# Attention with seven of a quad's 64 blocks of exponentials taken as transposes of computed blocks

## The reference, cut to what matters

```python
heads = x.reshape(Bs, Ss, H, D)                      # H = 16, D = 8, Ss = 4096
qkv = _qz_ring(heads + rx_theta)
q = jnp.transpose(qkv, (0, 2, 1, 3))
scores = jnp.einsum('bhsd,bhtd->bhst', q, q) / np.sqrt(D)
attn = jax.nn.softmax(scores, axis=-1)
ctx = jnp.einsum('bhst,bhtd->bhsd', attn, q)
```

## Time and profile before

| | us |
|---|---|
| median of 3 runs | 8488.46 (8488.23 to 8497.59) |
| span of the profiled execution | 8347.0 |
| main stage, first to last exponential (of the span) | 595.3 to 8088.5 |
| ACT busy | 7572.6, 91% |
| PE busy | 7391.0, 89% |
| DVE busy | 3996.2, 48% |

### The profile page before, as it was taken

One profiled execution on the slowest core, in us unless ns is written; L12 is line 12 of the kernel. 1 busy time (PEld: TensorE's weight loads), 2 busy tenths in 40 slices (PEclk: granted clock), 3 DMA queues, 4 the chain that ended last, 5 costly groups with the idle time before them and its releaser, 6 DMA issues. The chain is left out here.

```text
span 8347.0 us, 169002 instructions
## 1 busy us (share of the span) xinstructions
PE 7391.0 (89%) x59247; PEld 2074.5 (25%) x59247; DVE 3996.2 (48%) x15349; ACT 7572.6 (91%) x6026; POOL 1120.4 (13%) x1165
## 2 busy tenths in 40 slices
PE   6558998889889999999999999999999988898987
PEld 3542221122212222222222222222222222121224
DVE  6984333333335555555555555555553343232553
ACT  2339999999999999999999999999999999999971
POOL 2742111111111111111111111111100000000000
PEclk8779999999999999999999999999999999999998
DMA  6752111111111111121112111111100010000018
GB/s 204 210 149 66 47 47 45 47 52 49 45 46 54 54 53 53 47 56 52 54 46 56 54 50 50 53 53 53 53 24 11 10 22 10 9 11 8 21 49 257
DMA packets 508316, 485.88 MB, mean 58 GB/s; under 512 B 229673, under 2 KB 411753, under 8 KB 506994
## 3 DMA queue, kind: packets, MB, share of 16 engines
q0 software_dynamic: 92880, 304.42, 12.5%
q1 hardware_dynamic: 414626, 170.83, 8.0%
HBM read 401.79 MB, written 73.33 MB: 57 GB/s over the span
## 5 line engine op out<-in xcount | busy, mean ns | idle before, releaser
L999 ACT ACTIVATE e<-sc 128x1536 f32<-128x1536 f32 x5376 | 7282.9, 1704 | 116.7 <-PE sc L928 115.4
L947 PE MATMUL acc<-e,v_cur 128*9 128x512 f32 x32256 | 4305.2, 598 | 30.5 <-DVE acc_sb L879 30.5
L928 PE MATMUL sc<-b_unit,a_cur 32*128 32x512 f16 x16384 | 2164.4, 386 | 544.6 <-ACT e L999 525.3
L928 PEld LDWEIGHTS sc<-b_unit,a_cur 32*128 32x128 f16 x16384 | 537.3, 91 | 4434.3 <-ACT e L999 4074.6
L605 POOL DMA_INDIRECT corners<-table,idx_st x873 | 835.0, 956 | 4728.4 <-ACT e L999 4417.2
L947 PEld LDWEIGHTS acc<-e,v_cur 128*9 128x9 f32 x32256 | 487.2, 89 | 974.9 <-issue 941.8
L629 DVE SCALAR_TENSOR_TENSOR val<-corners,w_st,val 128x128 f32<-128x128 f32 x2619 | 712.2, 345 | 7.7 <-DVE f_lg L1129 2.9
L879 DVE COPY acc_sb<-acc 128x512 f32<-128x512 f32 x129 | 89.1, 690 | 861.2 <-PE acc L947 843.4
L652 DVE TENSOR_TENSOR t_out<-misc,xt 128x128 f32<-128x128 f32 x96 | 28.0, 292 | 672.3 <-PE misc L708 637.1
L550 PE MATMUL cf_ps_t<-ident,cf_val 128*128 128x128 f32 x1152 | 160.0, 306 | 199.2 <-DVE cf_val L455 183.8
L416 POOL DMA_INDIRECT cf_corners<-table,cf_idx x288 | 285.2, 990 | 253.0 <-DVE cf_idx L441 148.5
(11 more groups left out here) (393 smaller groups left out, 4837.6 us busy)
## 6 DMA issues: line engine op xcount, KB each, us to landing
table<-pix SPq DMA_DIRECT2D x8, 2304.0 KB, 13.7
corners<-table,idx_st POOLq DMA_INDIRECT x873
ew<-in_ew SPq DMA_DIRECT2D x12, 1024.0 KB, 7.8
ew<-in_ew SPq DMA_DIRECT2D x48, 256.0 KB, 6.7
x_ch<-in_x SPq DMA_DIRECT2D x4, 2048.0 KB, 9.6
qn<-q SPq DMA_DIRECT2D x64, 128.0 KB, 2.5
ctx<-ctx_t SPq DMA_DIRECT2D x128, 64.0 KB, 1.8
out<-e_exp SPq DMA_DIRECT2D x32, 256.0 KB, 2.1
```

The lines of the kernel that those rows point to most:

```text
L928: last = self.nc.tensor.matmul(self.sc[k % self.SC][:, i, :], self.a[rows, t * P:(t + 1) * P], self.bst[u % 2][rows, :], start=True, stop= ...
L947: last = self.nc.tensor.matmul(self.acc[32 * h:32 * h + self.E1, :], self.v[:, t, h, :], self.e_of(j)[:, i, :], start=(t == 0), stop=(t == ...
L999: self.nc.scalar.activation(self.e_of(j)[:], self.sc[k % self.SC][:, 0:width, :], ACT.Exp, scale=1.0 / HD ** 0.5).then_inc(self.exp_done, 1)
```

## The change

For each quad, block (unit u, keys of chunk u+1), u = 0 to 6, is computed and kept, and block (unit u+1, keys of chunk u) is made from it and no longer computed. A new class `Plan` lays out the quad: 912 slabs in 304 steps of three, without tails; unit starts at steps 0, 43, 80, 118, 155, 192, 230, 267. The kept block is computed in two halves of three steps each (`e_kept`). `shuffle_sp` moves each half by 16 DMAs of 32 partitions x 8 slabs x 128 elements (128 KB) between quadrants into `e_turned`; `turn_dve` transposes it in 4 instructions of 128x1024 in 32x32 blocks, in place. Four turned groups stand at places 7, 9, 11 and 13 of the next unit's groups and read `e_turned` in runs of 32 elements. The ring of `e` has 5 buffers instead of 7. To make room, the convolution's weights and indices go to DRAM in the first stage and come back tile by tile (`rows_sp`), the `b` operand has one quad instead of two, and some buffers share memory. The items keep their order; `spread` maps their old positions to the new steps.

```diff
+    UNITS, PARTS, SC, WIDE, RING = UNITS, 4, 2, 3, 5
+    T_AT = (7, 9, 11, 13)
+            if u < UNITS - 1:
+                s0 = len(self.slabs)
+                n0 = next(n for n in ((9, 8, 7) if u else (3,)) if (s0 + 4 * n) % self.WIDE == 0)
+                kept = [self.GROUP * (u + 1) + t for t in range(self.GROUP)]
+                for i, n in enumerate((n0, 10)):
+                    order += left[:n]
+                    left = left[n:]
+                    self.halves[u, i] = (s0 + 4 * len(order)) // self.WIDE
+                    order += kept[2 * i:2 * i + 2]
+            order += left
+            self.slabs += [(u, t, h) for t in order for h in range(4)]
+            groups = [("direct", t) for t in order]
+            if u:
+                for bo, at in enumerate(self.T_AT):
+                    groups.insert(at, ("turned", bo))
...
+    def _before(self, k):
...
+            earlier = [k2 for k2 in self.slot if self.slot[k2] == self.slot[k]]
+        now = [k2 for k2 in earlier if k2 < k]
+        if now:
+            return self._last_use(max(now)) + 1
...
+    def spread(self, starts, old, items):
+        got, last = {}, -1
+        for at, item in sorted(items, key=lambda x: x[0]):
+            i, k = divmod(at, old)
+            if i + 1 < len(starts):
+                k = k * (starts[i + 1] - starts[i]) // old
+            k = max(last + 1, starts[i] + k)
...
+    def shuffle_sp(self, sp, qd, u, half):
+        done = qd * self.QUAD_STEPS + (self.plan.halves[u, half] + 3 + self.SC)
+        if half == 0:
+            used = self.plan.last_turned(u) + 1 if u else self.plan.last_turned(UNITS - 1) + 1 - UNITS * self.UNIT
+            sp.wait_ge(self.pv_done, qd * (UNITS * self.UNIT) + (self.PV_START + used))
+        sp.wait_ge(self.exp_done, done)
+        for a in range(4):
+            for c in range(4):
+                dst = self.turned[32 * c:32 * c + 32, a, half, :]
+                src = self.kept[32 * a:32 * a + 32, 0:self.KEPT, c * P:(c + 1) * P]
+                sp.dma_start(dst.rearrange("p (s x) -> p s x", x=P), src).then_inc(self.shuffled[half], 16)
+    def turn_dve(self, dve, qd, u, half):
+        dve.wait_ge(self.shuffled[half], qd * (self.BLOCKS * 16 * self.SHUFFLES) + (16 + 16 * self.SHUFFLES * (u + 1)))
+        for a in range(4):
+            x = self.turned[:, a, half, :]
+            last = self.nc.vector.transpose(x, x)
+        last.then_inc(self.half_turned, 1)
...
     def quad_pe(self, pe, qd, background, follows):
...
-            ready = sum(self.exp_for(g) <= k - self.SC for g in range(UNITS * self.UNIT))
-            at_once = UNITS * self.UNIT if u == UNITS else 0 if k in background else 1
-            for _ in range(max(min(ready - done, at_once), ready - done - self.PV_BEHIND)):
+            ready = sum(x <= k - self.SC for x in plan.ready)
+            at_once = total if over else 0 if k in background else 1
+            needed = max(background[k][0] if k in background else 0, plan.before.get(k - 1, 0))
+            for _ in range(max(min(ready - done, at_once), ready - done - self.PV_BEHIND, needed - done)):
...
     def quad_act(self, act, qd, between=lambda: None):
...
+            if k in plan.before:
+                act.wait_ge(self.pv_done, qd * (UNITS * self.UNIT) + (self.PV_START + plan.before[k]))
+            if k in plan.kept_step:
+                u, half, i = plan.kept_step[k]
+                if i == 0:
+                    blocks = u + half
+                    act.wait_ge(self.shuffled[1 - half], qd * (self.BLOCKS * 16 * self.SHUFFLES) + (16 + 16 * self.SHUFFLES * blocks))
...
         def conv_quad(qd, with_ffn, m0, first=False):
...
                 finish(qd, 2 * p)
+                if p:
+                    at.turn_dve(dve, qd, 2 * p - 1, 1)
                 conv.sample_dve(dve, n + LEAD, 1, st, 0)
...
                 conv.sample_dve(dve, n + LEAD + 1, 0, st, 3)
+                at.turn_dve(dve, qd, 2 * p, 0)
                 conv.turned_dve(dve, 2)
...
                 finish(qd, 2 * p + 1)
+                at.turn_dve(dve, qd, 2 * p, 1)
                 if not final:
                     at.staged_dve(dve, qd + 1, p)
...
         def ffn_quad(qd, with_ffn, m0, with_choice):
...
                 finish(qd, u)
+                if u:
+                    at.turn_dve(dve, qd, u - 1, 1)
```

More of the change, by code:

```diff
@@ L769, in __init__ @@
         self.nc, self.d, self.r, self.misc = nc, d, r, misc
+        self.plan = Plan()
+        self.QUAD_STEPS = self.plan.steps
         self.qn = sb("qn", [P, TILES, 4 * HD])
@@ L772, in __init__ @@
         self.a_next, self.a = (sb(n, [P, TOK], F16) for n in ("a_next", "a_cur"))
[L773 removed]
+        self.b = sb("b_all", [P, TOK], F16)
         self.v_next, self.v = (sb(n, [P, TILES, 4, HD + 1]) for n in ("v_next", "v_cur"))
         self.bst = [sb(f"b_unit{s}", [P, CHUNK], F16) for s in range(2)]
[L777 to L779 removed]
+        self.e = [sb(f"e{i}", [P, self.WIDE, CHUNK]) for i in range(Plan.RING)]
+        self.kept = sb("e_kept", [P, 9, CHUNK])
+        self.turned = sb("e_turned", [P, 4, 2, self.KEPT * P])
         self.acc_sb, self.rs = sb("acc_sb", [P, CHUNK]), sb("rs", [P, 16])
@@ L1318, in _ @@
     def _(sp):
+        for s in range(2):
+            conv.rows_sp(sp, LEAD, s)
         for p in range(at.PARTS - 1):
@@ L1323, in _ @@
         sp.sem_inc(at.ctx_stored[1], 16)
+        for half in range(2):
+            sp.sem_inc(at.shuffled[half], 16)
         conv.before_store_sp(sp, LEAD - 1)
@@ L1349, in conv_quad @@
                     at.store_ctx(sp, qd, 2 * p - 1)
+                if not (first and p == 0):
+                    at.shuffle_sp(sp, qd, 2 * p, 0)
+                    conv.rows_sp(sp, n + LEAD + 1, 1)
                 if with_ffn:
                     store_gate(m0 + p)
+                at.shuffle_sp(sp, qd, 2 * p, 1)
+                if first and p == 0:
+                    conv.rows_sp(sp, n + LEAD + 1, 1)
+                conv.rows_sp(sp, n + LEAD + 2, 0)
                 at.store_ctx(sp, qd, 2 * p)
+                if p < QPAIRS - 1:
+                    for half in range(2):
+                        at.shuffle_sp(sp, qd, 2 * p + 1, half)
                 conv.store_sp(sp, n + LEAD)
             sp.wait_ge(conv.stored, (n + 1) * 48)
-            sp.sem_inc(q_there, 1)
+            sp.sem_inc(r.passed, 1)
             at.load_q(sp, qd + 1, QPAIRS - 1)
@@ L1372, in ffn_quad @@
                     store_gate(m0 + with_ffn.index(u))
+                if u < UNITS - 1:
+                    for half in range(2):
+                        at.shuffle_sp(sp, qd, u, half)
+                if u in with_ffn:
                     ffn.store_sp(sp, m0 + with_ffn.index(u))
@@ L1382, in last_quad @@
             store_gate(FFN_PAIRS)
+            for half in range(2):
+                at.shuffle_sp(sp, qd, 0, half)
             for u in range(1, UNITS):
@@ L1392, in last_quad @@
                     ffn4.store_sp(sp, m - 1)
+                if u < UNITS - 1:
+                    for half in range(2):
+                        at.shuffle_sp(sp, qd, u, half)
+                if u > 1:
                     ffn4.store_gx_sp(sp, m - 1 - FFN4_FIRST, 4 * (m - 1) + AHEAD)
@@ L1413, in _ @@
         sp.wait_ge(conv.stored, (PAIRS - LEAD) * 48)
+        for s in range(2):
+            sp.wait_ge(conv.rows_in[s], (PAIRS - LEAD + 2 - s) * 32)
         sp.wait_ge(ffn.stored, FFN_PAIRS * 16)
@@ L1446, in _ @@
         dve.sem_inc(conv.val_ready, 2)
-        for s in range(2):
-            conv.stage_dve(dve, LEAD, s)
         at.init_dve(dve)
```

399 lines of the change are left out of this document (247 added, 152 removed).

## The result

| | before | after |
|---|---|---|
| median | 8489.17 us (8488.23 to 8497.59) | 9604.41 us (9595.19 to 9625.62) |
| ratio | | 1.1316, 95% interval 1.13 to 1.1332 |

The account below looks back on a forecast made before the run. The prediction took the kernel as bound by ACT with PE close behind, step by step. Span 8347 - 860 (steps that go) + 646 + 120 + 220 = 8473, with 141 around it 8614 us; range 8250 to 8900.

Parts of the forecast that it names:

- late steps: Main stage: ACT's step k needs a group that PE issues at k+1; 404 steps at 1.60 us extra, 646 us.
- groups at k itself: Another 0 to 60 positions a quad where the group is issued at k; up to 0.1 us each, range 0 to 90.
- DVE's transposes: 896 new DVE transposes make copies that free the misc bank late: 332 us in all, two thirds taken, 220; bounds 60, 360.
- shuffles: DMAs moving kept halves were to land before the exponentials of half 1: 0 us taken, bounds 0 and some 500.
- bursts, PE's own work: PE positions holding two groups (268) or a group and an item (350): 120 us taken, bounds 0 and 220.
- four places: PE's waits for DVE's misc bank copies: after `finish`, before `turned_dve(2)`, before `staged_dve`, in `ffn_quad`; 2.7, 4.3, 4.4, 6.1 us late.
- PE's total remains near ACT's: Claim for the main stage: PE's work stays near ACT's but lies in bursts behind place 7; 120 us taken.
- 10.3 fits barely: Half 0's 16 DMAs take 8.2 us and land some 2 later, against 8 steps (10.7 us) in unit 4.
- the fifth (the clock): Rival: a tenth of the main stage's groups run at 1.2 GHz, 350 us, 8960 in all; chance 0.05.
- The third, full price: Rival: nothing overlaps; bursts 190, DVE 332, positions k 90 us, 8886 in all; chance 0.14.
- The fourth (shuffles at half pace): Rival: 16.4 + 2 us against 8 to 13 steps, 500 us in all, half overlapping: about 9000; chance 0.06.
- The first and second: Rivals: ACT's count decides, 7940, chance 0.10; PE's idle time in long steps swallows bursts and DVE's lateness, 8370, chance 0.23.

Follow-up runs that it names:

- at their position: The changed kernel with PE issuing a group that exponential k waits for at position k, not k+1: 8932.71 us, 1.0511 of the kernel before.
- a position earlier: The changed kernel with PE issuing groups one position ahead of the step that waits for them (also called early groups): 8862.30 us, 1.0423 of before.
- small transposes: The changed kernel with 128x128 instead of 128x1024 transposes, output wrong: 9167.93 us; in the chain, with groups a position earlier too: 8090.16 us.
- small shuffles: The changed kernel with shuffle DMAs of one slab instead of eight, output wrong: 9535.02 us; in the chain, on top of the other two cuts: 7954.84 us.
- The stalls added to the kernel before: The kernel before with 400 steps where PE waits one exponential longer and issues a group before the scores: 9222.34 us, 1.0873 of before.
- all cuts: The changed kernel with groups a position earlier, small transposes and small shuffles together, output wrong: 7954.84 us, 0.9554 of before.
- the moved transposes: The changed kernel with groups a position earlier, transposes moved in DVE's list and three places mended, nothing left out: 8465.78 us, 0.9969 of before.

## Why the prediction was wrong

The floor of the sum is 7493 - 860 = 6633 us of main stage; the 640 steps went as counted, to 4864 exponentials, but no run came down to it. Over it the forecast had 986 us, and the change has 8616 - 6633 = 1983. The chain of runs takes this apart, by main stages, one cut after the other:

| term | forecast | main stages | over before | by |
|---|---|---|---|---|
| late steps | 646 | 662 | 677 | change to "at their position" |
| groups at k itself | 0 (range to 90) | 63 | 72 | to "a position earlier" |
| DVE's transposes | 220 (60 to 360) | 652 | 608 | to small transposes |
| shuffles | 0 (to 500) | 155 | 135 | to small shuffles |
| bursts, PE's own work | 120 (0 to 220) | 451 | 483 | what is left over the floor |

The first column of measurements is from one execution a run and crosses from the slower chips to the quicker one at the third row; the second takes each run against before on its own chip and is the better one where they differ. What a cut gives depends on its place in the chain.

**The late steps** were right in list, count and price: 404 of 2.94 us against 405 long waits that went, 1.68 us of time for each where 1.60 was forecast. The stalls added to the kernel before say the same of the mechanism.

**The step that failed most is "I take two thirds, 220; bounds 60 (short transposes) and 360":** the price of DVE's lateness, measured at 443 alone and 608 once the late steps are gone, above even the upper bound. The transposes' own duration was right (1.213 us, 896 times, against 1.22). What was wrong is what followed from lateness. I listed four places and gave each its lateness less 1.0 us of cover. PE's waits for DVE alone come to 318 us of the 443. The stall at step 191 shows what is added to them: after it PE works at 1.2 GHz, so the item and the group that come next are slow as well. DVE's own wait for a half that has not landed was not in the list either (323 us), but it stayed at 345 when the 443 went, so it is not what cost them. Quads 1 to 3, for which the list had one place and 9.5 us each (10 by its own 3 x 3.4), lose 26 each (458 to 463 us with early groups, 432 to 435 with small transposes too); quads 4 to 11 lose some 52 each where it had 28.5. The forecast's "part lies beside the long steps" was right in kind: the transposes cost 165 us more once those are gone. By the moved transposes, 395 of the 608 us (366 to -29 over before) come back without any work left out; that figure holds the other moves of those edits too, and 213 stay.

**Bursts: "PE's total remains near ACT's"** is where one sum was not made. In the earlier trace rows PE is busy for 436.8 us of quad 11. Take away the scores of 40 steps at 0.44 us (1.30 for scores and group less 0.86) and 419 are left, against ACT's 408. So PE has more work than ACT in eight quads, and all cuts together left 441 us there. Against the lengths of before less 40 x 1.343 = 54 us a quad, the eight quads hold 210 of the 451 us. The rest lies where PE is not the fuller engine: 96 in quads 12 to 14, 55 in quad 0 (ACT stands 34 us for shuffles there), 49 in quads 1 to 3, 42 in quad 15. For quads 12 to 14, with all cuts:

```profile
5895.00:7220.00 1325.00, 1212.19 (x9751) 283.39 (x9747) 501.20 (x2077) 1242.01 (x915) 0.00 (x0) 0.98 0.09 21
```

ACT is busy 1242 of 1325 us and PE 1212. So the missing sum explains less than half of this term, and bursts cost more than forecast even where the sum was right.

**Shuffles.** 16 DMAs took 8.2 us in SP's queue in the forecast, from DMAs of 256 KB. Here they take longer:

```profile
5293.31 11.72 SPq L1020 DMA_DIRECT2D e_turned<-e_kept  x16
```

"10.3 fits barely" was 3.5 us short. 2 MB in 11.72 us is 179 GB/s. As long as all else was late, most of this was hidden (76 us alone, 135 in the chain). The Trainium skill (SBUF — State Buffer, Door 1: The DMA port swizzle) would make it 9.6 us, an estimate from its 218 GB/s for 32 partitions. The row is slower than that, but gathers ran beside it: in 5294 to 5300 the core moved 234 GB/s in all. So it agrees with the direction and does not test the price.

**Of the rivals**, the fifth (the clock) was real but not at the size it was given: the main stage's granted clock of 0.91 means that the lower level holds 2 x 0.09 = 18% of it, 1550 us, against 150 before. What that costs was not isolated in the changed kernel. An estimate from the added stalls: there 2 x 0.02 x 8240 = 330 us more at the lower level (430 before the clock is rounded) went with 70 us of time, about 0.2 each, so 1400 us more would be some 250 to 300. More than 543 it can hardly be: by so much longer is PE busy with the same list of matmuls (53,578 and 53,570 of them in the traces) in the change (7141 us) than with all cuts (6598). These are not beside the table's terms but inside them: the clock rose along the chain (0.94 with the late steps gone, 0.97 with small transposes too, 0.98 with all). The third, full price, was the nearest, but even its 332 for DVE and 190 for bursts were too low (608 and 483). The fourth (shuffles at half pace) did not happen. The first and second are refuted: neither bursts nor DVE were swallowed.

The signs asked for: quads 4 to 11 longer (yes, 566), waits for `acc` near 400 times (753 in all, and of the long ones 405 by the runs that removed them), quads 1 to 3 and 12 to 14 shorter (no; DVE's lateness costs 26 us in each of quads 1 to 3, and PE stood 64 us for the copy ahead of the gate, 13 times, and 18 with small transposes), transposes of 1.2 us (yes), ACT waiting for DMAs at kept steps, which was to count against the forecast (yes, 35 times, 109 us).

**What stays open:** the clock's own share was not separated from the stalls that lower it; some 125 us of what the transposes cost alone, and 264 of the 608, are not PE's waits for DVE and were not taken apart; and the 451 us of the last row were split by quads, not by an experiment. That PE's bursts are their cause is argued.

## What to carry to other kernels

When work is taken off the engine that bounds, add up each other engine's busy time per stage as it will be, from the windows, before pricing anything else: here 419 us of PE against ACT's 408, in eight quads of 16, said that there was little left to absorb a stall. A new instruction on a half idle engine costs above all by its place (here up to 395 of 608 us): look at which shared buffer's release stands behind it in that engine's order, and move it behind that. And a ring that is short by one position can be mended in the issuing order without removing any work (749 us here); had both been done, the change would have been worth 0.3% instead of costing 13%.

## What the runs showed of the hardware

- Chips differ: the same program took 8496 us (median) on one and 8332 on another. Two executions of it, 8488 and 8347 us long, had their first exponential at 727 and 595 us (162 against 208 GB/s between 100 and 400 us, in a stretch of indirect gathers). Their main stages agree within 10 us (7503 and 7493), though quad 0 took 500 against 471.
- The 32x32 transpose on DVE moves 128x1024 fp32 in 1213 ns and 128x128 in 280 (means of 896): 1.04 ns for each element of a lane and 0.15 us beside.
- Short stalls lower TensorE's clock: 400 added steps, in which PE stood for example 0.81 and 1.42 us, brought a stage at 0.99 to 0.97. At the lower level, in the change, the eight matmuls of a product took 2.07 us instead of 1.16.
- 32-partition DMAs between SBUF quadrants, 128 KB each, take 0.62 us each in SP's queue (median of 3584), and 16 in a row 11.72 us where gathers ran beside them.
